# Long convolution by pairs of channel chunks, its step split around the scan of h, and the input transpose moved, in a GRU kernel

## The reference

```
x1 = x + conv(x, cond)                     # 16 taps, each channel by itself
for t in 0..255:
    gi = x1[t] @ W_ih + b_ih;  gh = h @ W_hh + b_hh
    r = sigmoid(gi_r + gh_r);  z = sigmoid(gi_z + gh_z)
    n = tanh(gi_n + r * gh_n)
    h = (1 - z) * n + z * h
    out[t] = x1[t] + h
```

## Time and profile before

| | us |
|---|---|
| runs of the kernel, median of 3 | 1025.09 (1024.73 to 1025.14) |
| profiled execution, span from first to last instruction | 1023.1 |
| TensorE matmuls busy | 1015.2 |
| TensorE weight loads busy | 808.1 |
| VectorE busy | 865.7 |
| ScalarE busy | 398.5 |
| GpSimd busy | 237.9 |

### The profile page before, as it was taken

The page is one execution under the profiler, slowest core; times in us unless marked ns, Lnnn a source line. Parts: engine busy times, 40 slices in busy tenths (PEclk is TensorE's granted clock), DMA queues, the critical chain, the costliest instruction groups (busy, mean ns, idle before and its releaser), DMA issues.

```text
span 1023.1 us, 58102 instructions
## 1 busy us (share of the span) xinstructions
PE 1015.2 (99%) x24838; PEld 808.1 (79%) x24838; DVE 865.7 (85%) x2851; ACT 398.5 (39%) x1816; POOL 237.9 (23%) x784
## 2 busy tenths in 40 slices
PE   8999999999999999999999999999999999999997
PEld 5878888888787888888888888888888888888875
DVE  7788888888898888888888898888888887777555
ACT  5334333433433343333434333333433343333433
POOL 3222222222222222222222222222222222222222
PEclk9999999999999999999999999999999999999999
DMA  8721001010100101001010010101001000000000
GB/s 297 72 35 39 19 21 31 15 36 19 29 25 12 35 19 34 24 11 36 15 39 19 15 36 11 39 19 28 22 15 35 14 29 16 11 29 4 20 19 13
DMA packets 66994, 32.07 MB, mean 31 GB/s; under 512 B 44464, under 2 KB 65584, under 8 KB 66736
## 3 DMA queue, kind: packets, MB, share of 16 engines
q1 hardware_dynamic: 66304, 28.25, 10.8%
q10 hardware_dynamic: 432, 0.11, 0.0%
HBM read 19.86 MB, written 8.49 MB: 28 GB/s over the span
## 4 chain that ended last, share of the span: by engine, by line
PE 97%; issue 1%; POOL 1%; DVE 0%; DMA 0%; ACT 0%; DVEq 0%; POOLq 0%
PE pg L334 65%; PE pg L324 32%; POOL tz L283 1%; PE pcv L362 0%; DMA cnd<-cond 0%; DVE hp L570 0%; DVE gn L549 0%; POOL nzh L296 0%; DVE an L557 0%; POOL cpad L273 0%; POOL nzh L280 0%; POOL cpad L275 0%; POOL rz L278 0%; POOL zcp L279 0%; ACT nzh L472 0%
## 5 line engine op out<-in xcount | busy, mean ns | idle before, releaser
L334 PE MATMUL pg<-whh,hp 128*32 128x192 f32 x16368 | 713.0, 326 | 2.2 <-ACT whh L461 1.1
L334 PEld LDWEIGHTS pg<-whh,hp 128*32 128x32 f32 x16368 | 531.2, 110 | 137.7 <-DVE hp L570 4.2
L324 PE MATMUL pg<-wih,x 128*32 128x192 f32 x8192 | 381.3, 326 | 0.0
L296 POOL TENSOR_TENSOR nzh<-rz,hp 128x32 f32<-128x32 f32 x512 | 158.2, 309 | 780.1 <-ACT rz L467 780.1
L467 ACT ACTIVATE rz<-gt 128x64 f32<-128x64 f32 x512 | 136.3, 266 | 483.7 <-DVE gt L545 458.9
L324 PEld LDWEIGHTS pg<-wih,x 128*32 128x32 f32 x8192 | 265.5, 110 | 65.8
L512 DVE SCALAR_TENSOR_TENSOR x<-xb,cnd,x 128x512 f32<-128x512 f32 (+1 forms) x420 | 294.8, 702 | 7.9
L570 DVE TENSOR_TENSOR_SCAN hp<-zcp,nzh 128x96 f32<-128x96 f32 x512 | 173.6, 339 | 41.6 <-ACT nzh L472 41.3
L545 DVE STREAM_TRANSPOSE gt<-pg 128x128 f32<-128x128 f32 x512 | 160.2, 313 | 49.4 <-PE pg L334 42.0
L557 DVE TENSOR_TENSOR_SCAN an<-rz,gn 128x64 f32<-128x64 f32 x512 | 149.2, 291 | 51.9 <-ACT rz L467 51.7
L472 ACT ACTIVATE nzh<-an 128x32 f32<-128x32 f32 x512 | 120.6, 236 | 126.9 <-DVE an L557 126.9
(11 more groups left out here) (47 smaller groups left out, 47.4 us busy)
## 6 DMA issues: line engine op xcount, KB each, us to landing
xb<-x SPq DMA_DIRECT2D x96, 94.0 KB, 2.0
out<-x SPq DMA_DIRECT2D x60, 128.0 KB, 1.9
wih<-w_ih SPq DMA_DIRECT2D x4, 768.0 KB, 8.0
whh<-w_hh SPq DMA_DIRECT2D x4, 768.0 KB, 14.6
xw<-x SPq DMA_DIRECT2D x24, 64.0 KB, 3.5
xb<-x SPq DMA_DIRECT2D x16, 62.0 KB, 1.9
tz<-taps SPq DMA_DIRECT2D x12, 64.0 KB, 3.5
xs<-x SPq DMA_DIRECT2D x1, 512.0 KB, 4.7
```

Source lines behind the costliest of these rows:

```text
L296: pool.tensor_tensor(nzh[:, f, ::2, :, 1], chunks(rz[:, f, 1, :, 1]), h_of(t - 1, slice(f * CH, (f + 1) * CH)), ALU.mult).then_inc(s_zh[f], 1)
L324: i = pe.matmul(pg[m % Q][f][D * j:D * (j + 1), RZ:END], x1_of(c, 2 * m, 2 * m + 2), wih[:, c, :, :].rearrange("p (g k) (j d) -> p j g k d ...
L334: i = pe.matmul(pg[t // 2 % Q][f][D * j:D * (j + 1), 0:IN], hp[:, t % 2, 2 * c + 1 - t % 2:2 * c + 3 - t % 2, :, 1].rearrange("p u b -> p ...
```

## The change

The change has these parts.

- `inputs`: in step t the transpose of the input products is that for t+2; before it was that for t+3, with two in step 0 and none in step 250.
- The transpose stands ahead of half 0's `scan_n`; before it stood between half 1's `scan_n` and half 1's `scan_h`.
- The long convolution takes two chunks at a time. In each of its 32 steps it does one lag for an even chunk, over all columns (`WHOLE`), and the same lag for the odd chunk beside it in two halves of the columns (`LEFT`, `RIGHT`). `LEFT` stands ahead of half 1's `scan_h`, `WHOLE` and `RIGHT` behind it. Each waits on its own predecessor, one step earlier.
- The wait counts of `s_long` on TensorE and SP follow the new number of operations, 96 a stretch, and `arriving` loads the chunks at other steps: relative to the first step of a stretch's 32, chunk 0 is due at 0, chunk 1 at -3, chunk 2 at 16, chunk 3 at 13 (before: 0, 8, 16, 24), and the loads are issued 6 to 2 steps ahead of that.
- The long convolution's operations now come ahead of `spread` and `early` in the text of the loop.

```diff
         def inputs(t):
-            if t == 0:
-                return range(2, 4)
-            if t < T - 6:
-                return range(t + 3, t + 4)
-            return range(t + 2, min(t + 3, T)) if t > T - 6 else range(0)
+            return range(t + 2, min(t + 3, T))
...
-        EVERY = [(lag, c) for c in range(C) for lag in range(K)]
+        TAPPED = [(pair, lag) for pair in range(C // 2) for lag in range(K)]
+        LEFT, WHOLE, RIGHT = 0, 1, 2
+        LONGS = 3 * len(TAPPED)
 
         def arriving(k, c):
-            at = SPANS[k][0] + W2 // C * c
+            at = SPANS[k][0] + K * (c // 2) - 3 * (c % 2)
             return (at - 3, at - 1) if k == c == 0 else (at - 6, at - 2)
...
                 if i == 0 and k >= 2:
-                    sp.wait_ge(s_long, len(EVERY) * (k - 2) + K * (c + 1))
+                    sp.wait_ge(s_long, LONGS * (k - 2) + 3 * K * (c // 2 + 1))
...
                     elif 2 * m >= LONG[0][0]:
-                        pe.wait_ge(s_long, len(EVERY) * sum(a <= 2 * m for a, _ in LONG))
+                        pe.wait_ge(s_long, LONGS * sum(a <= 2 * m for a, _ in LONG))
...
-            def long(k, q):
-                lag, c = EVERY[q]
+            def long(k, i, part):
+                pair, lag = TAPPED[i]
+                c = 2 * pair + (part != WHOLE)
                 a, b = LONG[k]
+                half = (b - a) // 2 * B
+                lo, hi = {LEFT: (0, half), WHOLE: (0, 2 * half), RIGHT: (half, 2 * half)}[part]
                 if lag == 0:
                     dve.wait_ge(s_xb[k][c], 16 * PIECES)
-                if q == 0 and b > KEEP:
+                if i == 0 and part == LEFT and b > KEEP:
                     for n in range(max(a - KEEP, 0) // TB, (b - 1 - KEEP) // TB + 1):
                         dve.wait_ge(s_out[n], 16 * C)
                 if lag:
-                    dve.wait_ge(s_long, len(EVERY) * k + q)
-                o, xx, n = x1_of(c, a, b), window(k), b - a
-                now = xx[:, c, (K - 1) * B:(K - 1 + n) * B]
-                dve.scalar_tensor_tensor(o, xx[:, c, (K - 1 - lag) * B:(K - 1 - lag + n) * B],
+                    dve.wait_ge(s_long, LONGS * k + 3 * (i - 1) + part + 1)
+                o, xx = x1_of(c, a, b)[:, lo:hi], window(k)
+                now = xx[:, c, (K - 1) * B + lo:(K - 1) * B + hi]
+                dve.scalar_tensor_tensor(o, xx[:, c, (K - 1 - lag) * B + lo:(K - 1 - lag) * B + hi],
                                          cnd[:, c, K - 1 - lag:K - lag],
                                          o if lag else now, ALU.mult, ALU.add).then_inc(s_long, 1)
+
+            def tapped(t):
+                return [(k, t - at) for k, (at, to) in enumerate(SPANS) if at <= t < to]
...
             for t in range(T):
                 transpose_rz(t, 0)
                 transpose_n(t, 0)
+                for i in inputs(t):
+                    transpose_in(i // H, i % H)
                 scan_n(t, 0)
                 transpose_rz(t, 1)
                 transpose_n(t, 1)
                 scan_h(t, 0)
                 scan_n(t, 1)
-                for i in inputs(t):
-                    transpose_in(i // H, i % H)
+                for k, i in tapped(t):
+                    long(k, i, LEFT)
                 scan_h(t, 1)
+                for k, i in tapped(t):
+                    long(k, i, WHOLE)
+                    long(k, i, RIGHT)
                 for c, steps in TURNED.items():
                     for q in share(NT, steps, t):
                         spread(c, q)
                 for lag in share(K, EARLY, t):
                     early(lag)
-                for k, steps in enumerate(SPANS):
-                    for q in share(len(EVERY), steps, t):
-                        long(k, q)
```

## The result

| | median, us | runs | ratio to before, 95% interval |
|---|---|---|---|
| before | 1025.09 | 6, 1024.56 to 1025.69 | |
| changed kernel | 1028.27 | 6, 1027.63 to 1028.79 | 1.003 [1.0019, 1.004] |
| changed kernel, repeated on another occasion | 1027.62 (before there: 1024.92) | 8, 1027.13 to 1027.93 | 1.0025 [1.0015, 1.0036] |

The change makes the kernel 2.7 to 3.2 us slower. The profiled execution took 1027.63 us with a span of 1025.9; before's span was 1023.1. So 2.8 us are to be found in the trace, and the page gives no hint of where. Its first line has busy time by engine, as the earlier trace rows.

The account below looks back on a forecast made before the run. TensorE's chain of matmuls, 3.90 us a step, was taken as the bound; five parts at 0 each left the span at 1023.1 us, 1025.1 by the median, range 1024.3 to 1026.6.

Parts of the forecast that it names:

- Part 1: Input transpose moved ahead of half 0's scan of n: its product never waits and it falls into a gap; price 0.
- Part 5: The ends: TensorE's last steps wait for half 0's scan, not touched; -0.5 to +0.2 us, taken as 0.
- the low odds of "slower": Whole kernel: a chance of 0.05 for slower, against same 0.93 and faster 0.02.
- Parts 2 and 3: Half multiply-add ahead of half 1's scan of h (0 to 0.11 us late) and 0.21 us more VectorE work a step; price 0.
- slack of half 1's scan: Middle steps: half 1's scan of h could end 0.39 us later before TensorE waits, its limit 0.76 into the step.
- the rival at 1065: VectorE becomes the bound through its added 0.21 us a step, 40 us in all; 1 in 100.
- other signs given: Changed profile: steps of 3.90 us, scan h 0.35 to 0.5 behind the new half, the head transpose waiting for TensorE mid-loop.
- The 3.2 us: From 986 us on, TensorE's weight loads waited 10 times for h, 3.2 of its 7.9 us idle.
- Part 4: Chunk order and loads: an earlier piece may delay column 2's last xw load at the start; 0 to 1.5 us once, taken as 0.
- a wait at 48 us: Start, step 6: TensorE waiting for xw there would show the prediction wrong; late-load rival up to 1.5 us, 12 in 100.
- The rival on GpSimd: GpSimd's z*h held by the new half, making half 1's scan of h 0.43 us late; 8 us, 1033; 4 in 100.

Follow-up runs that it names:

- older_only: Kernel before with input transposes one product older (t+2 in each step), left at their old place behind half 1's scan of n: 1024.81 us, ratio 0.9998.
- load_later: Changed kernel with chunk 1's window for the first stretch loaded at steps 7 and 8, not 3 to 6: 1027.56 us, ratio 1.0024.
- move_only: Kernel before with only the change's input schedule and input transpose place, nothing of the convolution: 1027.91 us, ratio 1.0028.
- conv_only: Changed kernel with the input schedule and transpose place of before, so only the convolution's part: 1024.99 us, ratio 1.0.
- two_halves: Kernel of both edits with the odd chunk's second half also ahead of half 1's scan of h: 1032.85 us, ratio 1.0074.
- even_before: Kernel before with four chunks of products in every step (THIN = T): 1026.55 us, ratio 1.0014.
- both: Changed kernel with steps 251 to 253's input transposes at their old place and chunk 1's first window loaded at steps 7 and 8: 1024.36 us, ratio 0.9994.

## Why the prediction was wrong

**The step that failed is the first of Part 1.** It says that TensorE has finished the product for t+3 before step t begins, so that the transpose for t+2 never waits. That holds while four chunks are made in a step. In the thinned steps the lead melts by one chunk a step, and from step 251 on it is used up. The rows showed TensorE's last steps, the kernel's text gave THIN, and the old schedule changed its form at step 250, just there; I costed that difference as one transpose that falls into a gap. The sentence was false for the kernel before as well: before step 249, 1009 chunk products have been made, and its transpose for t+3 reads 1012. No wait showed there because the transpose stood late in the step, which older_only bears out. Against the 0 of the prediction the runs show 2.5 to 2.9 us for this alone (load_later and move_only, over before), and the traces 3.0 between step 20 and the last add.

**Part 5** repeats the error: it says that the last steps' chain is "not touched". The transpose was put into that very chain. The bound given there, -0.5 to +0.2, and the low odds of "slower" hung on the same sentence; no rival had the transpose waiting.

**Parts 2 and 3 held.** Scan h starts 0.01 us behind the start of TensorE's step in both kernels, so it has not moved, where 0 to 0.11 was given. The long operations behind it free VectorE before the next transpose, which now waits 0.28 in the middle. conv_only bears the price of 0 out. The slack of half 1's scan was read 0.05 too large, which changed nothing here. VectorE's busy time was off: I gave 40 to 45 us more, and the page shows 5.8 (871.5 against 865.7). Two groups of the changed kernel by form (busy, mean ns, idle before), as the earlier trace rows:

```profile
L513 DVE SCALAR_TENSOR_TENSOR x<-xb,cnd,x 128x256 f32<-128x256 f32 x390 | 182.8, 469 | 0.0
...
L513 DVE SCALAR_TENSOR_TENSOR x<-xb,cnd,x 128x512 f32<-128x512 f32 x180 | 130.6, 726 | 0.0
```

By duration a step has 0.726 + 2 x 0.469 = 1.66 where it had 1.48, close to the 1.69 said, and over all forms the durations of the long operations add up to 355.8 us against 314.0, 41.8 more. But the new operations overlap their neighbours more, and busy time counts an overlap once. A bound worked out from added durations (the rival at 1065) is too dear for that reason among others: two independent operations of 512 and 256 take 1.12 together, less than their 1.20. Above all VectorE is not the bound here, as the unchanged step shows.

Of the other signs given, the step of 3.90, the 0.38 from the new half to scan h and the transpose that waits for TensorE came true. TensorE's weight loads waited for h 7.0 us in all, and not the 4 to 5 at most; that sign pointed to the loss at the end. The 3.2 us that the prediction called TensorE's idle time in the last steps were also such waits of weight loads, most of them under running matmuls: the matmuls of the kernel before waited for h there once, for 0.81 us.

**Part 4** gave the xw load 0 to 1.5 us with 0 as likeliest. The traces have 0 to 1.1 of idle weight loads, and the medians 0. The range was right, though a wait at 48 us, which the changed kernel's trace shows, was given as a sign of being wrong; that it happens without the early load too was not foreseen.

**The rival on GpSimd** fell. The half starts at 503.54 while GpSimd's operation runs from 503.37 to 503.68; the half takes its 0.46, where the mean of all 390 is 0.469, and GpSimd the 0.31 that it took in the kernel before. Neither was held, and scan h, which needs GpSimd's result, starts on time. The Trainium skill, SBUF — State Buffer, Who interferes with whom, would have one of the two wait; here the measurement decides.

## What to carry to other kernels

When an operation is moved forward in a step or given older data, work out for every phase of the loop, the first and the last steps included, when what it reads is ready; a schedule that is thinned or capped at the end shifts that by a little more in each step. In an in-order queue the price of such a wait is not the moved operation's but that of everything behind it, here the recurrence itself. And slack given to an engine that is not the bound is worth nothing until the bound's own work gets shorter.

## What the runs showed that I had not expected

- A multiply-add that depends on the one just ahead of it on VectorE costs about 0.1 us more than an independent one. Two dependent ones of 256 columns took 0.98 in the kernel before, two independent ones 0.86 in two_halves. The row of two_halves stands with that experiment (504.71); this one is of the timeline of before:

```profile
909.51 0.98 DVE L512 SCALAR_TENSOR_TENSOR x<-xb,cnd,x 128x256 f32<-128x256 f32 x2
```

- All kernels with the new convolution end sooner after their last add. From its start to the issue of the last store they take 0.22 us, and from there to the end 2.0 to 2.1; before, older_only, move_only and even_before take 0.34 to 0.36 and 2.2 to 2.5. It is most of what both is ahead of before. By their traces it is 0.52 of 0.7 us. No run was made on its cause, and it stays open.
